# A graph layer on one core: GpSimd takes a row buffer back at VectorE's addition in place of TensorE's matmul

## The reference

```python
h = jnp.maximum(_layernorm(x, axis=-1), 0.0)
hx = jnp.einsum('ni,rio->rno', h, weight)              # 8 weights of 256 x 256
msg = hx[edge_type, src]
agg = jax.ops.segment_sum(msg, dst, num_segments=num_nodes)
x + agg * 0.5 ** 0.5 + h_bias + (h @ loop_weight) * 0.5 ** 0.5
```

## Time and profile before

| | |
|---|---|
| median of 3 runs | 2552.59 us |
| the runs | 2552.97, 2542.56, 2552.59 us |
| span of the profiled execution | 2587.3 us |
| the profiled execution's time outside its span | not given by the page |
| mean granted TensorE clock | 0.814 of full speed |
| main loop, first to last gather | 212.6 to 2561.7 us |
| DMA | 290.10 MB, mean 112 GB/s |

### The profile page before, as it was taken

The page is one execution under the profiler, slowest core; times in us unless marked ns, Lnnn a source line. Parts: engine busy times, 40 slices in busy tenths (PEclk is TensorE's granted clock), DMA queues, the critical chain, the costliest instruction groups (busy, mean ns, idle before and its releaser), DMA issues.

```text
span 2587.3 us, 36344 instructions
## 1 busy us (share of the span) xinstructions
PE 1645.8 (64%) x10568; PEld 1254.5 (48%) x10568; DVE 1297.6 (50%) x4142; ACT 345.3 (13%) x427; POOL 1552.6 (60%) x1646
## 2 busy tenths in 40 slices
PE   0002657766776777777777577667667777767767
PEld 0001445555554555555555455555455555545556
DVE  3273454455454555555455455455544554545444
ACT  2163010110111011011011011111111110111110
POOL 7704666666665666666666666666665666666663
PEclk9999778787877887787887787787787787777779
DMA  6554333333333333333333333333333333333332
GB/s 232 178 194 150 95 107 98 109 108 99 108 108 101 105 107 107 102 108 105 105 105 105 98 106 105 107 105 104 106 101 105 106 105 105 106 99 107 106 107 70
DMA packets 133929, 290.10 MB, mean 112 GB/s; under 512 B 34511, under 2 KB 77387, under 8 KB 130655
## 3 DMA queue, kind: packets, MB, share of 16 engines
q0 software_dynamic: 78624, 214.80, 29.0%
q10 hardware_dynamic: 49922, 54.25, 6.5%
q1 hardware_dynamic: 5180, 18.71, 2.2%
HBM read 262.02 MB, written 25.60 MB: 111 GB/s over the span
## 4 chain that ended last, share of the span: by engine, by line
PE 50%; DVE 18%; another core or an unknown queue 15%; issue 12%; DMA 2%; DVEq 1%; ACT 0%; POOL 0%; POOLq 0%; SPq 0%; ACTq 0%
PE psum L958 32%; PE psum L1022 15%; DVE room L825 10%; DVE onehot L751 3%; DMA h_table<-room 2%; PE psum L963 2%; PE psum L1008 1%; DVE stats L614 1%; DVE result L776 1%; DVEq L813 1%; DVE raw_onehot L748 1%; DMA room<-x 1%; DVEq L825 0%; ACT psum L476 0%
## 5 line engine op out<-in xcount | busy, mean ns | idle before, releaser
L410 POOL DMA_INDIRECT rows<-h_table,src_i x1542 | 1459.5, 946 | 978.3 <-issue 483.2
L825 DVE TENSOR_TENSOR room<-room,psum 128x256 f32 x1661 | 694.6, 418 | 1085.2 <-remote 502.1
L958 PE MATMUL psum<-w_sb,room 128*128 128x256 f32 x3104 | 1081.9, 469 | 161.8 <-DVE result L776 87.9
L1022 PE MATMUL psum<-onehot,rows 128*128 128x128 f16 x6260 | 711.1, 241 | 543.2 <-issue 329.5
L1022 PEld LDWEIGHTS psum<-onehot,rows 128*128 128x128 f16 x6260 | 515.9, 108 | 837.6 <-issue 449.2
L958 PEld LDWEIGHTS psum<-w_sb,room 128*128 128x128 f32 x3104 | 632.0, 231 | 245.6 <-issue 110.3
L751 DVE TENSOR_SCALAR onehot<-lane,base_i 128x128 f16<-128x128 f16 x1565 | 437.2, 280 | 66.4 <-DVE room L825 1.6
L499 ACT COPY room<-zeros 128x2048 f32<-128x2048 f32 x94 | 178.4, 1898 | 1874.7 <-DVE result L779 1099.2
L963 PE MATMUL psum<-w_sb,own_hT 128*128 128x256 f32 x384 | 129.6, 420 | 9.4 <-issue 9.3
L1063 PE MATMUL psum<-unfit_p,ones 128*1 128x6 f32 x2 | 0.2, 170 | 201.6 <-DVE room L656 201.6
L399 POOL DMA_INDIRECT raw<-x,src_i x96 | 92.1, 959 | 31.1 <-issue 28.9
(11 more groups left out here) (68 smaller groups left out, 254.4 us busy)
## 6 DMA issues: line engine op xcount, KB each, us to landing
rows<-h_table ACTq DMA_DIRECT2D x2944, 1.0 KB
rows<-h_table,src_i POOLq DMA_INDIRECT x1542
own<-h_table ACTq DMA_DIRECT2D x97, 128.0 KB
own_x<-x ACTq DMA_DIRECT2D x97, 128.0 KB
out<-result ACTq DMA_DIRECT2D x97, 128.0 KB
room<-x SPq DMA_DIRECT2D x12, 1024.0 KB
h_table<-room ACTq DMA_DIRECT2D x12, 1024.0 KB
w_sb<-weight SPq DMA_DIRECT2D x2, 1024.0 KB
```

The source lines that it names most:

```text
L410: nc.gpsimd.indirect_dma_start(out=rows[:, q % NB, :], out_offset=None, in_=table[:, :], in_offset=bass.IndirectOffsetOnAxis(ap=src_i[:, c ...
L825: nc.vector.tensor_tensor(window, window, sum_of(c).rearrange("p (a w) -> p a w", w=W), ALU.add).then_inc(added, 1)
L958: nc.tensor.matmul(ps_out[:, 0:D], nodes[:, m, :], w_sb[:, h, r, :], start=(m == 0), stop=False)
L1022: last = nc.tensor.matmul(sum_of(c)[:, h * P:(h + 1) * P], now[:, part * D + h * P:part * D + (h + 1) * P], onehot[:, k, :], start=(part = ...
```

## The change

The wait of a group of four gathers is on `added`, no longer on `summed`, for the same chunk. The count is the same, as both semaphores rise by one for each chunk, raw chunks and ScalarE's chunks included. Nothing else is changed, and the order of instructions on every engine is as before.

```diff
             def gather(q):
                 if q >= NB and (q - NB) % NB_STEP == 0:
-                    pool.wait_ge(summed, gathered[q - NB + NB_STEP - 1] + 1)
+                    pool.wait_ge(added, gathered[q - NB + NB_STEP - 1] + 1)
                 c = gathered[q]
```

## The result

| | before | changed |
|---|---|---|
| median of the runs | 2552.78 us (4 runs) | 2723.63 us (4 runs) |
| lowest, highest | 2542.56, 2559.06 | 2716.49, 2727.3 |
| ratio to before, 95% interval | | 1.067 (1.0641 to 1.07) |
| span of the profiled execution | 2587.3 us | 2718.4 us (own time 2720.24) |

The changed kernel is slower by 171 us, 6.7%. I had forecast no change with a chance of 0.63, and 0.17 for any loss; the range ended at 2573. The kernel before took 2550 to 2580 us in some sessions on a chip and 2079 us in others, on one and the same chip too (chip 9), and never both within a session; only the first kind shows common stalls of TensorE, VectorE and ScalarE, and the comparison above fell in it. I call them sessions with and without stalls.

What follows compares the result with a forecast made beforehand. No engine filled the loop; the last-ending chain ran over TensorE (50%), VectorE (18%), issue and unknown waits, without GpSimd. The terms summed to 0 on the path, giving 2551 us, just under the median; the range was 2530 to 2573.

Steps and rivals of the forecast that it cites:

- What bounds the kernel: Chunk loop: no engine fills it, gathers are on no part of the path, GpSimd's 435 us of waits are for buffers.
- The lead: Gathers ahead of TensorE's matmuls: 12.0 us at the 1093rd, 8.4 us at the smallest; rows need 2.1 us to land.
- Least and most delay of a release: Gathers released by VectorE's addition L825 come 0.4 to 0.6 us later at least, 4.6 us at the worst found.
- TensorE meets its rows as early as now: 381 waits x 0 = 0 us.: Waits before every fourth gather: the lead covers their delay, so 0 us; without it 230 us and more.
- The rival of longer common stalls: VectorE's "remote" waits: longer gather runs stretch the stalls, 5% of 388 us giving 2571 us; chance 0.15.
- One-hots: VectorE's L751 beside gathers: at most 7 us of the path to gain or 62 us to lose; taken as 0.

Runs made afterwards that it cites:

- 14 buffers: Kernel before with 14 row buffers in use in place of 18; 2545.72 us against 2552.17 with stalls, ratio 0.996.
- the groups of eight: Kernel before with one wait for eight gathers in place of four, still on TensorE's sum; 2548.82 us against 2550.56 with stalls, ratio 1.0.
- per-gather waits: Changed kernel with a wait on VectorE's addition before every gather, not every fourth; 2600.82 us with stalls, ratio 1.0174.
- the run meant to separate it: Changed kernel with a double wait per four gathers: TensorE's sum, and VectorE's addition four chunks earlier; 2079.81 us without stalls, ratio 0.9998.
- per-gather kernel on sums: Kernel before with a wait on TensorE's sum before every gather; 2572.58 us against 2580.41 with stalls (0.9972), 2078.27 us without (0.9995).

## Why the prediction was wrong

- *What bounds the kernel.* Right that no gather lies on the path and that GpSimd waits for buffers. Unread was why it waits: I took 435 us of pauses for slack. In sessions without stalls GpSimd has no pauses, so they were there because the stalls kept the others behind. The wait for buffers came to 597 us and not to some 490.
- *The lead.* Right in what it was for: TensorE's wait for rows is 15.0 and 15.1 us, and 14 buffers (four chunks later) cost nothing. The numbers were less good: the 1093rd gather is 14.3 us ahead, outside the 8 to 12 that I gave, the 35th 6.1 us for the 7.3 expected, and the smallest lead is 4.6 us at the 38th, less than the 6.1 us that I had kept as an upper bound for landing. TensorE did not wait for it.
- *Least and most delay of a release.* Right in size (0.4 to 4.6 us were expected): after a stall the gather starts 1.89 us after the first addition at the mean, 2.88 in the stall shown and 4.9 at most, for 0.36 at the mean before.
- *"TensorE meets its rows as early as now: 381 waits x 0 = 0 us."* The step that failed. That TensorE would not wait held; that the path would therefore be as long as now did not. The sum put the effect of the new wait on the common stalls at nothing (only the rival below had it, at 20 us), and this term is what was measured: 297 stalled waits, each 0.75 us longer at the mean (3.54 for 2.79), 173 us in all.
- *The rival of longer common stalls.* The right place (VectorE's "remote" waits, up by 185 us, over the 20 us that I named as the sign) and the right observation that a stall ends about 2 us after GpSimd's last gather. Wrong was the reason against it, "GpSimd gets no more room than now": it looked at the release inside a stall alone, while the restart behind it comes 1.5 us later. Wrong were the price, 5% of 388 us where VectorE's remote waits rose by 37%, and with it the range. Its proposed cause, merged pauses, fell with the groups of eight.
- *One-hots.* Right that they hardly matter: 11 ns shorter at the mean, 18 us of VectorE's time, in the direction of a gain. The one-hots that start 0.4 to 0.7 us into a gather are fewer, 212 for 366. Wrong was that a gather blocks its second half: those that start later than 0.7 us into it keep 255 ns.
- *What I could have seen.* The first phase of the kernel before already showed the other engines slow while GpSimd gathers (groups of up to 43 us against 8). Read that way, a change to when GpSimd gathers can have a price with no wait in between, and 0.15 for the rival was too little.

**What is shown and what is not.** Shown: the loss goes with longer stalled waits of VectorE, in sessions that have stalls; a later release by the old signal costs nothing; merging pauses with the old signal costs nothing; per-gather waits bring the new signal from 6.7% to 1.7%, and the same waits on sums are at -0.3%. Not shown is why the new signal makes a stall longer. The feedback orders the kernels by how late GpSimd restarts, but it was read from these traces, its link over free buffers does not fit them, and the run meant to separate it met no stalls. Only 63% of the stalled waits before and 54% in the changed kernel end with GpSimd paused, so a pause is one way out and not the only one. What in a session makes the stalls stays open, too. Slower DMA traffic is not seen: the packets of GpSimd's gathers last 153 ns at the mean in the kernel before and 152 in the per-gather kernel on sums without stalls.

No version beats both kernels by much: with stalls 14 buffers take 0.996 and per-gather waits on sums 0.9972 of the kernel before, and without stalls both take the same 2079 us.

## What to carry to other kernels

A wait that delays only a transfer with ample lead can still cost: here 6.7%, with TensorE's wait for rows unchanged. Look for stretches where several engines slow down together, and ask what runs through them. Look at the signal before the number of buffers: four buffers fewer cost nothing, while a signal that let GpSimd go on 1.5 us later after a stall cost 6.7%, though why is not shown. Take the kernel before along in every session: here one and the same kernel took 2550 and 2079 us, and a change of 6.7% was there only in the one.

## What the hardware showed that I had not expected

- In sessions with stalls TensorE, VectorE and ScalarE slow down together while GpSimd gathers unbroken at 1.25 us a gather: TensorE's matmuls at 1308.40 and 1310.48 are 2 us apart with nothing to wait for, a group of the first phase takes 43 us for 8. A stall that ends with GpSimd paused ends 1.7 us after GpSimd's last gather at the median (1.9 in the changed kernel). The gathers themselves keep their 946 ns.
- Sessions without stalls ran the same kernel in 2079 us for 2553, with a mean granted clock of 0.88 to 0.89 for 0.81 to 0.83, and with GpSimd as the bound. The clock explains little of it: the costliest matmuls (L958) take 469 ns in the kernel before and 447 in the per-gather kernel on sums without stalls, and 3104 x 22 ns are 68 of the 474 us.
- A one-hot on VectorE that starts 0.4 to 0.7 us into a gather is held until about the gather's end (350 ns at the mean for a start at 0.4 to 0.5 us, 410 at 0.5 to 0.6, 312 at 0.6 to 0.7), and one that starts earlier or later keeps 255 ns; the whole effect is 39 us of VectorE's time before and 22 us after (14 ns x 1565).
